# Weighting two heads in one VectorE instruction, with four buffers for counts and weighted tiles

## The chip, the cores and the metric

The kernel runs on one NeuronCore of one Trainium2 chip. The time is the device time of one execution in microseconds; several executions are made and their median is given. The engines are named as in the profile: PE is TensorE (PEld its weight loads), DVE is VectorE, ACT is ScalarE, POOL is GpSimd, SP is SyncE, which issues the DMAs.

## What is computed

The reference is one layer over x of 16 sequences x 512 tokens x 128 channels, float32: a normalised and modulated input goes through a gathering convolution, then a mixture of 8 experts of which each token takes 2. The part that matters here is the convolution. Each token and each of 8 heads has a frequency and a phase, and takes 32 taps of the sequence at fractional positions, each weighted by an entry of a table of 64 bins that is computed from the token itself:

```python
offs = phase[..., None] + freq[..., None] * taps          # 32 taps
pos = jnp.clip(jnp.arange(L)[None, :, None, None] + offs, 0.0, L - 1)
i0 = jnp.floor(pos).astype(jnp.int32); frac = pos - jnp.floor(pos)
g0 = xh[b_idx, i0, h_idx]
g1 = xh[b_idx, jnp.minimum(i0 + 1, L - 1), h_idx]
gathered = g0 + frac[..., None] * (g1 - g0)
kmat = (x @ kernel_w.T + kernel_b).reshape(B, L, H, 64)
w = jnp.take_along_axis(kmat, bins, axis=3)               # bins from offs
y = jnp.einsum('blhs,blhsd->blhd', w, gathered)
```

After it come the output product, the residual, the second normalisation, the gate (softmax over the two best of 8 scores), the experts (silu(h1) * h2, then the second product) and the residual again.

## The kernel before

The kernel doesn't gather. For each token and head it forms a dense row over the 512 positions: how many taps lie below each position and how far the next one is, as a product of a few parameter rows with constants. This row is weighted by the token's bins and multiplied by the steps of the input along the sequence.

Sequences are worked in 8 pairs. A pair has 8 rounds (R counts them, r = R % 8), one for each residue of the token index; 128 partitions hold 64 tokens of each of the two sequences. A round has 8 heads (h), and one head of one round is a tile T, 512 in all. Tile T passes through these steps:

- TensorE, `tile_on(T)`: two bfloat16 products of 512 columns, `ps_n` (L984) and `ps_p` (L987), each with two PSUM banks. They wait until the count and the gap of tile T-2 have read the banks.
- ScalarE, `gap(T)`: Relu of `ps_p` with a scale for each token, into `ee` (L771), two buffers.
- VectorE, `counted(T)`: `dq = ps_n * 2^27 + ee`, rounded to int32 (L1291), two buffers.
- VectorE, `weighted(T)`: `aw = dq * ks` over 65 groups of 8 positions, 520 elements, where `ks` holds one weight for each group and is read with a stride of zero within the group (L1301). `aw` has three buffers (`RING`).
- TensorE, `turn_tile(T)`: four transposes of 128x128 into `ps_t` (L995), two banks.
- ScalarE, `tile_evicted(T)`: copy into `att` (L779).
- TensorE, `weigh(R, g)`: 16 products for four heads, into `ps_y` (L1015).

Each engine has its own queue, written out by hand, and semaphores between them. No engine goes round a waiting instruction. The order in which the loops issue, for each T:

- TensorE: `tile_on(T + 3)`, `turn_tile(T)`, then what belongs to this head: `counts` of the next round (h 0, L976), `bins` (h 1, L952) and `weigh` of the last round (h 1), `weigh_edges` (h 2, L1024), `weigh` (h 5), products of the neighbouring pairs of sequences at h 3, 5 and 7 (such as `waves`, L947, `scores`, L1042, `outputs`, L1034), and two `turn_edges` (h 7, L1002).
- ScalarE: `gap(T + 3)`, `tile_evicted(T)`, then `counted` (h 0, L761), `copied` (h 4, L794), groups of four normalising activations (L729) at r 1 and 2, h 0 and 2, evictions of side products (L714, L739, L743, L748) at h 0, 4 and 6, and two `edge_evicted` (h 7, L786).
- VectorE: `counted(T + 1)`, `weighted(T)`, then `binned` (h 3, L1281), `edge_terms` (h 5, L1310) and the statistics, scores and masks of the neighbouring pairs of sequences.
- SyncE loads `ks` for round R + 2 once all weightings of round R are done; GpSimd pads bins, finishes normalisations and scatters rows, its scatters paced by the count of weightings (`s_aw`).

Two waits of VectorE matter for the change. `counted(T)` waits for `s_aw >= T - 1`, that is for the weighting of tile T-2, since it writes the same `dq` buffer. `weighted(T)` waits for the transposes of tile T-3, which read the same `aw` buffer.

After the head loop the expert stage runs over 135 slot tiles and the results are fetched and stored. It uses `aw` as space for other tiles.

Of the kernel before, what the change touches and what calls it, by code (L numbers as in the profile page):

```python
# [5 lines left out]
HEADS, D, TAPS, BINS = 8, 16, 32, 64  # L6
P = 128
# [7 lines left out]
NG = L // 8 + 1  # L15
NX = 8 * NG
# [4 lines left out]
ROWS = 32  # L21
QUAD = P // ROWS
KRING = 4
RING = 3
AHEAD = 3
SCALE = 2.0 ** 27
EXPERTS, FF = 8, 256
# [48 lines left out]
UNIT = {tag: n for n, tag in enumerate(ORDER)}  # L76
# [12 lines left out]
def build(nc, x, wave_wT, wave_b, kern_wT, kern_b, out_wT, w12T, w3T, gateT, cT, wmod,  # L89
          c_n, c_p, c_e, c_tok, c_ident, c_iota, c_tri, c_id, c_trash, c_tile, out):  # L90
    fp32, bf16, i32, u32 = mybir.dt.float32, mybir.dt.bfloat16, mybir.dt.int32, mybir.dt.uint32
    ALU, ACT, AX = mybir.AluOpType, mybir.ActivationFunctionType, mybir.AxisListType

    def rows(ap, extra):

        return bass.AP(ap.tensor, ap.offset, [list(ap.ap[0])] + [list(e) for e in extra])
# [12 lines left out]
    with ctx:  # L109
        def sb(name, shape, dt=fp32):  # L110
            return ctx.enter_context(nc.sbuf_tensor(name, shape, dt))
# [4 lines left out]
        def sem(name):  # L116
            return ctx.enter_context(nc.semaphore(name))
# [49 lines left out]
        ka = sb("ka", [P, 2, HEADS, PADK])  # L167
        ks = sb("ks", [P, 2, HEADS, NG])
        ee = sb("ee", [P, 2, 512])
        dq = sb("dq", [P, 2, NX], i32)  # L170
        aw = sb("aw", [P, RING, NX])
        att = sb("att", [P, SLOTS, 512])
        yt = sb("yt", [P, RES, HALF * P])
# [63 lines left out]
        ps_n, ps_p, ps_t, ps_y, side = ps[0:2], ps[2:4], ps[4:6], ps[6], ps[7]  # L237
# [18 lines left out]
        s_dq, s_aw, s_at, s_ev, s_y, s_yy = (sem("tap_count_ready"), sem("weighted"), sem("turned"), sem("evicted"),  # L256
                                             sem("y_product"), sem("y_copied"))
# [629 lines left out]
        def _(pe):  # L887
# [101 lines left out]
            def turn_tile(T):  # L989
# [3 lines left out]
                for j in range(NJ):  # L993
                    o = RES - r + j * P
                    last = nc.tensor.transpose(bank[:, j * P:j * P + P], aw[:, T % RING, o:o + P], ident[:, :])  # L995
                last.then_inc(s_at, 1)
# [179 lines left out]
        def _(dve):  # L1176
# [16 lines left out]
            for a in (2, 5):  # L1193
                g = mod[:, a * C:a * C + C]
# [13 lines left out]
            def deviation(which, done):  # L1208

                fence()  # L1210
                for r in range(RES):
                    ins = nc.vector.bn_aggr(mv[:, which, r, :], stats[:, which, r, :])
                link(ins)
                nc.vector.tensor_tensor(var[:, which, :], rows(mv[:, which, 0, 1:2], [[2, RES]]), tiny[:, :], ALU.add).then_inc(done, 1)

            def first_spread(i, n):
                if n == 0:
                    dve.wait_ge(s_xl, 16 * (i + 1))
                    if i:
                        dve.wait_ge(s_h, i)  # L1220
                spread(0, xc[:, i % 3, :], n)

            def second_spread(i, n):
                dve.wait_ge(s_xo, 2 * i + n + 1)
                spread(1, xo[:, :, :].rearrange("p r c -> p (r c)"), n)
# [37 lines left out]
            def waves(i):  # L1263
                dve.wait_ge(s_sd, SIDE["wave", i] + 1)
                nc.vector.tensor_tensor(wv[:, :, :], side[:, 0:RES * 16].rearrange("p (r w) -> p r w", w=16),
                                        rows(wbias[:, :], [[0, RES], [1, 2 * HEADS]]), ALU.add).then_inc(s_wv, 1)

            def periods(i):
                dve.wait_ge(s_tanh, i + 1)
                half = (MAX_FREQ - MIN_FREQ) / 2  # L1270
                f = freq[:, :, :].rearrange("p r h -> p (r h)")
                link(nc.vector.scalar_tensor_tensor(f, f, half, middle[:, :], ALU.mult, ALU.add))
                nc.vector.reciprocal(rows(x3[:, 0, 0:1], [[3, TILES]]), f).then_inc(s_fa, 1)

            def binned(R):
                dve.wait_ge(s_sd, SIDE["bins", R] + 1)
                if R >= KRING:
                    dve.wait_ge(s_kf, R - KRING + 1)
                    dve.wait_ge(s_kst[(R - KRING) % RES], 16 * ((R - KRING) // RES) + 16)
                    dve.wait_ge(s_kd, R - KRING + 1)  # L1280
                nc.vector.tensor_tensor(kn[:, R % KRING, :, LO:LO + BINS], side[:, :].rearrange("p (h k) -> p h k", k=BINS),  # L1281
                                        kbias[:, :].rearrange("p (h k) -> p h k", k=BINS), ALU.add).then_inc(s_kn, 1)

            def counted(T):

                o = RES - T // HEADS % RES
                dve.wait_ge(s_n, T + 1)
                dve.wait_ge(s_e, T + 1)
                if T >= 2:
                    dve.wait_ge(s_aw, T - 1)  # L1290
                nc.vector.scalar_tensor_tensor(dq[:, T % 2, o:o + 512], ps_n[T % 2][:, :], SCALE, ee[:, T % 2, :], ALU.mult, ALU.add).then_inc(s_dq, 1)  # L1291

            def weighted(T):

                R, h = T // HEADS, T % HEADS
                if h == 0:
                    dve.wait_ge(s_ksl[R % 2], 32 * (R // 2 + 1))
                dve.wait_ge(s_dq, T + 1)
                if T >= RING:
                    dve.wait_ge(s_at, UNIT["tile", T - RING] + 1)  # L1300
                nc.vector.tensor_tensor(aw[:, T % RING, :].rearrange("p (g k) -> p g k", k=8), dq[:, T % 2, :].rearrange("p (g k) -> p g k", k=8),  # L1301
                                        rows(ks[:, R % 2, h, 0:1], [[1, NG], [0, 8]]), ALU.mult).then_inc(s_aw, 1)

            def edge_terms(R):

                dve.wait_ge(s_ev, UNIT["count", R] + 1)
                dve.wait_ge(s_kd, R + 1)
                if R >= 2:
                    dve.wait_ge(s_est[R % 2], 32 * (R // 2))
                nc.vector.tensor_tensor(kr[:, R % 2, :], en[:, R % 2, :], kd[:, R % 2, :], ALU.mult).then_inc(s_kr, 1)  # L1310

            def scaled(i, n):

                dve.wait_ge(s_sd, SIDE["out", i, n] + 1)
                dve.wait_ge(s_modld, 32 * (i + 1))
                if i:
                    dve.wait_ge(s_xo, 2 * i + n - 1)
                else:
                    dve.wait_ge(s_modst, 16)
                nc.vector.tensor_tensor(hn[:, 4 * n:4 * n + 4, :], side[:, :].rearrange("p (r c) -> p r c", c=C),  # L1320
                                        rows(mb[:, 2, :], [[0, 4], [1, C]]), ALU.mult).then_inc(s_hn, 1)
# [34 lines left out]
            for T in range(NT):  # L1356
                i, R, r, h = T // TILES, T // HEADS, T // HEADS % RES, T % HEADS
                last, more = i - 1, i + 1 < PAIRS
                if T + 1 < NT:
                    counted(T + 1)  # L1360
                weighted(T)
                if h == 3 and R + 2 < NR:
                    binned(R + 2)
                if h == 5 and R + 1 < NR:
                    edge_terms(R + 1)
                if more:
                    if (r, h) == (0, 1):
                        first_spread(i + 1, 0)
                    if (r, h) == (0, 2):
                        first_spread(i + 1, 1)  # L1370
                    if (r, h) == (0, 6):
                        deviation(0, s_rs1)
                    if (r, h) == (3, 1):
                        waves(i + 1)
                    if (r, h) == (3, 6):
                        periods(i + 1)
                if i:
                    if (r, h) == (0, 7):
                        scaled(last, 1)
                    if (r, h) == (1, 2):  # L1380
                        second_spread(last, 1)
                    if (r, h) == (1, 4):
                        deviation(1, s_rs2)
                    if (r, h) == (4, 0):
                        scores(last)
                    if (r, h) == (4, 2):
                        choices(last)
                    if (r, h) == (4, 4):
                        masks(last)
                    if (r, h) == (5, 1):  # L1390
                        ranks_read(last)
                    if (r, h) == (5, 2):
                        spotted(last, 0)
                    if (r, h) == (5, 3):
                        spotted(last, 1)
                if (r, h) == (7, 1):
                    scaled(i, 0)
                if (r, h) == (7, 5):
                    second_spread(i, 0)
# [27 lines left out]
            for k, d in enumerate((1, 2, 4)):  # L1427
                a, b = upto[:, k % 2, :], upto[:, 1 - k % 2, :]
# [44 lines left out]
            for f in range(PAIRS):  # L1473
                s = f % 2
# [74 lines left out]
```

## Time and profile before

| | us |
|---|---|
| median of three executions | 1491.42 |
| lowest and highest | 1490.12, 1495.94 |
| the profiled execution | 1488.08 |
| its span, first to last instruction | 1486.3 |
| TensorE busy in the span | 1196.9 |
| VectorE | 1049.9 |
| ScalarE | 924.4 |
| GpSimd | 718.3 |

The span is that of one profiled execution, and all durations are from it. Matmuls are pipelined and their ends are modelled, so the busy time of TensorE overstates its work. Idle time of an engine is listed ahead of the instruction that ended it, with what released it. The granted clock is a share of 2.4 GHz.

### The profile page before, as it was taken

The numbers are of one execution on the slowest core, as the hardware profiler recorded it, in microseconds if no ns is written. First come the engines' busy times: TensorE is split into PE (matmuls) and PEld (weight loads), VectorE is DVE, ScalarE is ACT, GpSimd is POOL, SyncE is SP. The second block draws the span as 40 slices with busy tenths as digits, with TensorE's granted clock in tenths as the row PEclk, the third lists the DMA queues.
The fourth block names the chain that finished last, engine by engine and source line by source line (L and its number), as shares of the span: only waits on it lengthen the run. The fifth ranks groups of instructions, "written<-read, shape, count | busy, mean of one in ns | idle before, by whom it ended". The sixth has DMA issues, their size and how long they took to land.

```text
span 1486.3 us, 35019 instructions
## 1 busy us (share of the span) xinstructions
PE 1196.9 (81%) x11339; PEld 769.4 (52%) x11339; DVE 1049.9 (71%) x2314; ACT 924.4 (62%) x1905; POOL 718.3 (48%) x930
## 2 busy tenths in 40 slices
PE   0589988898899898898989988898992399999950
PEld 0346655555565555555555555555652155565530
DVE  1388798888978887888888798878884233333336
ACT  0277777777677777777677777777770155555530
POOL 4253146348536644753573476255243645455430
PEclk9999999999999999999999999999996699999985
DMA  5345434544443454445445444544351253222227
GB/s 160 112 127 139 119 100 135 151 108 136 129 136 106 130 145 116 125 133 136 114 127 149 115 108 121 148 115 115 109 148 56 70 160 95 73 73 69 73 90 281
DMA packets 208737, 180.22 MB, mean 121 GB/s; under 512 B 147633, under 2 KB 177201, under 8 KB 208177
## 3 DMA queue, kind: packets, MB, share of 16 engines
q1 hardware_dynamic: 199888, 160.07, 38.4%
q0 software_dynamic: 8672, 17.92, 3.6%
q8 instruction: 96, 1.57, 0.5%
q14 instruction: 81, 0.66, 0.1%
HBM read 95.81 MB, written 82.12 MB: 120 GB/s over the span
## 4 chain that ended last, share of the span: by engine, by line
PE 47%; DVE 18%; issue 14%; ACT 9%; POOL 7%; DMA 4%; SPq 1%; DVEq 0%; ACTq 0%; POOLq 0%
DVE aw L1301 9%; PE ps L995 8%; PE ps L1138 7%; PE ps L1015 6%; PE ps L984 4%; ACT att L779 4%; PE ps L1153 3%; PE ps L987 3%; DVE dq L1291 3%; PE ps L952 3%; POOL slot_scratch L570 2%; ACT ee L771 2%; PE ps L1002 2%; PE ps L1145 2%; DMA att<-y_scratch 1%
## 5 line engine op out<-in xcount | busy, mean ns | idle before, releaser
L771 ACT ACTIVATE ee<-ps,f 128x512 f32<-128x512 f32 x512 | 354.7, 693 | 202.9 <-PE ps L987 200.6
L1291 DVE SCALAR_TENSOR_TENSOR dq<-ps,ee 128x512 int32<-128x512 f32 x512 | 352.7, 689 | 135.7 <-ACT ee L771 83.5
L1301 DVE TENSOR_TENSOR aw<-dq,ks 128x520 f32<-128x520 int32 x512 | 415.3, 811 | 1.2 <-DMA ks<-k_scratch 1.2
L995 PE MATMUL ps<-ident,aw 128*128 128x128 f32 x2048 | 323.2, 281 | 49.7 <-DVE aw L1301 30.6
L995 PEld LDWEIGHTS ps<-ident,aw 128*128 128x128 f32 x2048 | 237.6, 142 | 221.0 <-DVE aw L1301 132.1
L779 ACT ACTIVATE att<-ps 128x512 f32<-128x512 f32 x512 | 308.1, 602 | 21.2 <-PE ps L995 20.8
L984 PE MATMUL ps<-cn,ptt 128*128 128x512 bf16 x512 | 199.9, 390 | 38.9 <-DVE dq L1291 38.1
L601 POOL COPY kn<-kn 128x256 f32<-128x256 f32 x64 | 25.4, 397 | 390.9 <-DVE kn L1281 390.9
L987 PE MATMUL ps<-cp,ptt 128*128 128x512 bf16 x512 | 196.7, 384 | 0.0
L701 POOL DMA_INDIRECT y_scratch<-aw,idu x135 | 129.2, 957 | 129.3 <-ACT aw L875 128.1
L570 POOL DMA_INDIRECT slot_scratch<-hrow,spotu x128 | 133.6, 1044 | 81.2 <-DVE aw L1301 47.5
L1453 DVE TENSOR_TENSOR aw<-ee,ps 128x256 f32<-128x256 f32 x135 | 56.8, 421 | 136.6 <-ACT ee L862 135.6
L862 ACT ACTIVATE ee<-ps 128x256 f32<-128x256 f32 x135 | 51.7, 383 | 152.9 <-PE ps L1138 152.9
L1015 PE MATMUL ps<-att,dl 128*32 128x128 f32 x4096 | 143.5, 282 | 0.8
L1138 PE MATMUL ps<-kn,ee 128*128 x270 | 143.1, 612 | 0.1
L1015 PEld LDWEIGHTS ps<-att,dl 128*32 128x32 f32 x4096 | 107.7, 112 | 60.1 <-ACT att L779 36.4
L786 ACT ACTIVATE att<-ps 128x512 f32<-128x512 f32 x128 | 74.4, 599 | 48.2 <-PE ps L1002 47.9
L984 PEld LDWEIGHTS ps<-cn,ptt 128*128 128x128 bf16 x512 | 49.8, 97 | 98.5 <-DVE dq L1291 68.3
L1002 PE MATMUL ps<-ident,ka 128*128 128x128 f32 x512 | 76.0, 278 | 14.4 <-ACT att L779 14.0
L1153 PE MATMUL ps<-hg,aw 128*128 x540 | 82.5, 275 | 0.1
L1132 PE MATMUL ps<-ident,dl 128*128 128x128 f32 x135 | 38.3, 283 | 54.8 <-DMA dl<-slot_scratch 32.5
L608 POOL TENSOR_TENSOR kd<-kn 128x504 f32<-128x504 f32 x64 | 77.5, 1212 | 0.0
(175 smaller groups left out, 1689.8 us busy)
## 6 DMA issues: line engine op xcount, KB each, us to landing
k_scratch<-kn SPq DMA_DIRECT2D x64, 512.0 KB, 2.6
ka<-e_scratch SPq DMA_DIRECT2D x64, 512.0 KB, 3.9
ks<-k_scratch SPq DMA_DIRECT2D x128, 130.0 KB, 4.3
e_scratch<-kr SPq DMA_DIRECT2D x128, 126.0 KB, 3.5
dl<-slot_scratch SPq DMA_DIRECT2D x135, 65.0 KB, 1.8
att<-y_scratch SPq DMA_DIRECT2D x16, 512.0 KB, 5.1
xc<-in_x SPq DMA_DIRECT2D x8, 512.0 KB, 5.9
h_scratch<-hx SPq DMA_DIRECT2D x8, 512.0 KB, 5.1
```

The lines of the kernel that those rows point to most:

```text
L570: pool.indirect_dma_start(out=slots[:, :], out_offset=bass.IndirectOffsetOnAxis(ap=spotu[:, k * RES + r:k * RES + r + 1], axis=0), in_=hro ...
L701: pool.indirect_dma_start(out=yscr[:, :], out_offset=bass.IndirectOffsetOnAxis(ap=idu[:, s:s + 1], axis=0), in_=yrow[:, y, :], in_offset=N ...
L771: act.activation(ee[:, T % 2, :], ps_p[T % 2][:, :], ACT.Relu, scale=f27[:, i % 2, r, h:h + 1]).then_inc(s_e, 1)
L779: act.activation(att[:, h, :], ps_t[UNIT["tile", T] % 2][:, :], ACT.Copy).then_inc(s_ev, 1)
L984: nc.tensor.matmul(ps_n[T % 2][:, :], p, cn[:, h % QUAD, :], start=True, stop=True).then_inc(s_n, 1)
L987: nc.tensor.matmul(ps_p[T % 2][:, :], p, cp[:, h % QUAD, :], start=True, stop=True).then_inc(s_p, 1)
L995: last = nc.tensor.transpose(bank[:, j * P:j * P + P], aw[:, T % RING, o:o + P], ident[:, :])
L1015: last = nc.tensor.matmul(ps_y[ROWS * k:ROWS * k + ROWS, g * P:g * P + P], dl[:, R // RES % 2, j, h, :], att[:, h, j * P:j * P + P], start ...
L1138: nc.tensor.matmul(ps_h[j % 2][:, :], xT[:, j % 2, :], w12[:, bass.ds(experts[j % 8] * (2 * FF), 2 * FF)], start=True, stop=True).then_inc ...
L1153: last = nc.tensor.matmul(ps_z[j % 2][:, 0:C], hidT[:, j % 2, k * P:k * P + P], w3[:, bass.ds(experts[j % 8] * (HALVES * C) + k * C, C)], ...
L1291: nc.vector.scalar_tensor_tensor(dq[:, T % 2, o:o + 512], ps_n[T % 2][:, :], SCALE, ee[:, T % 2, :], ALU.mult, ALU.add).then_inc(s_dq, 1)
L1301: nc.vector.tensor_tensor(aw[:, T % RING, :].rearrange("p (g k) -> p g k", k=8), dq[:, T % 2, :].rearrange("p (g k) -> p g k", k=8), rows( ...
```

## The change

The weighting of an even tile and that of the following odd tile become one instruction, issued at the odd tile. `dq` has four buffers instead of two, `aw` four instead of three; with an even tile in slot s the odd one is in slot s + 1, so the pair is one access pattern, and `ks` is read for heads h and h + 1. The waits follow: the count of tile T waits for the weighting of tile T-4 (`s_aw >= T - 3`), the double weighting waits for the counts of both tiles and for the transposes of the tile four before the later one. The counter of weightings rises by two at once. TensorE, ScalarE, GpSimd and SyncE have the same instructions in the same order.

```diff
-RING = 3
+RING = 4
...
-        dq = sb("dq", [P, 2, NX], i32)
+        dq = sb("dq", [P, RING, NX], i32)
...
-                if T >= 2:
-                    dve.wait_ge(s_aw, T - 1)
-                nc.vector.scalar_tensor_tensor(dq[:, T % 2, o:o + 512], ps_n[T % 2][:, :], SCALE, ee[:, T % 2, :], ALU.mult, ALU.add).then_inc(s_dq, 1)
-
-            def weighted(T):
-
-                R, h = T // HEADS, T % HEADS
+                if T >= RING:
+                    dve.wait_ge(s_aw, T - RING + 1)
+                nc.vector.scalar_tensor_tensor(dq[:, T % RING, o:o + 512], ps_n[T % 2][:, :], SCALE, ee[:, T % 2, :], ALU.mult, ALU.add).then_inc(s_dq, 1)
+
+            def weighted_two(T):
+
+                R, h, s = T // HEADS, T % HEADS, T % RING
                 if h == 0:
                     dve.wait_ge(s_ksl[R % 2], 32 * (R // 2 + 1))
-                dve.wait_ge(s_dq, T + 1)
+                dve.wait_ge(s_dq, T + 2)
                 if T >= RING:
-                    dve.wait_ge(s_at, UNIT["tile", T - RING] + 1)
-                nc.vector.tensor_tensor(aw[:, T % RING, :].rearrange("p (g k) -> p g k", k=8), dq[:, T % 2, :].rearrange("p (g k) -> p g k", k=8),
-                                        rows(ks[:, R % 2, h, 0:1], [[1, NG], [0, 8]]), ALU.mult).then_inc(s_aw, 1)
+                    dve.wait_ge(s_at, UNIT["tile", T + 1 - RING] + 1)
+                nc.vector.tensor_tensor(aw[:, s:s + 2, :].rearrange("p a (g k) -> p a g k", k=8), dq[:, s:s + 2, :].rearrange("p a (g k) -> p a g k", k=8),
+                                        rows(ks[:, R % 2, h, 0:1], [[NG, 2], [1, NG], [0, 8]]), ALU.mult).then_inc(s_aw, 2)
...
                 if T + 1 < NT:
                     counted(T + 1)
-                weighted(T)
+                if T % 2:
+                    weighted_two(T - 1)
```

## Rows read from the trace of the kernel before

**Rows 1.** Stretch: length; busy us PE, PEld, DVE, ACT, POOL; clock; DMA share; GB/s.

```profile
350.00:500.00 150.00, 131.53 (x1386) 83.72 (x1384) 127.81 (x254) 110.53 (x215) 85.73 (x112) 0.98 0.46 131
```

**Rows 2.** Line L1301 alone: ns min/median/max, first and last start.

```profile
L1301 DVE TENSOR_TENSOR aw<-dq,ks x512: 682/690/2804, 68.7 to 1113.0; 128x520 f32<-128x520 int32 x171
```

**Rows 3.** Groups of instructions by line: busy us, mean ns, idle before, releaser.

```profile
L1301 DVE TENSOR_TENSOR aw<-dq,ks 128x520 f32<-128x520 int32 x512 | 415.3, 811 | 1.2 <-DMA ks<-k_scratch 1.2
...
L1291 DVE SCALAR_TENSOR_TENSOR dq<-ps,ee 128x512 int32<-128x512 f32 x512 | 352.7, 689 | 135.7 <-ACT ee L771 83.5 <-PE ps L984 26.0 <-DVE aw L1301 0.5
...
L1310 DVE TENSOR_TENSOR kr<-en,kd 128x504 f32<-128x504 int32 x64 | 57.3, 895 | 11.1 <-ACT en L761 11.1
```

**Rows 4.** Timeline of VectorE: start us, length us, instruction.

```profile
1099.48 0.69 DVE L1291 SCALAR_TENSOR_TENSOR dq<-ps,ee 128x512 int32<-128x512 f32 x1
1100.09 0.69 DVE L1301 TENSOR_TENSOR aw<-dq,ks 128x520 f32<-128x520 int32 x1
1100.91 0.69 DVE L1291 SCALAR_TENSOR_TENSOR dq<-ps,ee 128x512 int32<-128x512 f32 x1
```

**Rows 5.** Groups of VectorE with 256 and 512 elements a partition.

```profile
L1453 DVE TENSOR_TENSOR aw<-ee,ps 128x256 f32<-128x256 f32 x135 | 56.8, 421 | 136.6 <-ACT ee L862 135.6 <-issue 1.0
...
L1281 DVE TENSOR_TENSOR kn<-ps,kbias 128x512 f32<-128x512 f32 x64 | 43.7, 683 | 4.3 <-PE ps L952 4.3
```

**Rows 6.** Timeline of several engines: how one instruction hands over to the next.

```profile
640.89 0.39 PE L984 MATMUL ps<-cn,ptt 128*128 128x512 bf16 x1
...
641.53 0.69 ACT L771 ACTIVATE ee<-ps,f 128x512 f32<-128x512 f32 x1 [1.54 <-PE ps L987]
...
641.89 0.66 PE L995 MATMUL ps<-ident,aw 128*128 128x128 f32 x4 [0.40 <-DVE aw L1301]
...
642.58 0.86 DVE L1301 TENSOR_TENSOR aw<-dq,ks 128x520 f32<-128x520 int32 x1
642.59 0.60 ACT L779 ACTIVATE att<-ps 128x512 f32<-128x512 f32 x1 [0.37 <-PE ps L995]
...
643.08 0.59 ACT L714 ACTIVATE ht<-ps 128x512 f32<-128x512 f32 x1
...
643.49 0.66 PE L995 MATMUL ps<-ident,aw 128*128 128x128 f32 x4 [0.17 <-DVE aw L1301]
...
643.99 1.86 PE L947 MATMUL ps<-ww,ht 128*128 128x16 f32 x16
...
651.73 0.69 ACT L771 ACTIVATE ee<-ps,f 128x512 f32<-128x512 f32 x1 [1.68 <-PE ps L987]
...
652.50 0.69 DVE L1291 SCALAR_TENSOR_TENSOR dq<-ps,ee 128x512 int32<-128x512 f32 x1 [0.64 <-ACT ee L771]
...
653.11 1.10 DVE L1301 TENSOR_TENSOR aw<-dq,ks 128x520 f32<-128x520 int32 x1
```

**Rows 7.** Timeline: work of even heads that isn't a tile's own.

```profile
648.38 0.62 ACT L761 ACTIVATE en<-ps 128x504 int32<-128x504 f32 x1
...
652.06 0.65 PE L1024 MATMUL ps<-att,hg 128*32 128x128 f32 x16
...
652.63 0.39 PE L984 MATMUL ps<-cn,ptt 128*128 128x512 bf16 x1
...
655.64 0.39 ACT L794 ACTIVATE yt<-ps 128x256 f32<-128x256 f32 x1
...
611.58 0.89 ACT L729 ACTIVATE hx<-xc,shift,rstd 128x128 f32<-128x128 f32 x2
```

**Rows 8.** Stretches of 4 us, columns as in rows 1.

```profile
618.00:622.00 4.00, 2.17 (x14) 1.11 (x17) 3.97 (x10) 2.23 (x5) 3.92 (x6) 0.88 0.34 135
622.00:626.00 4.00, 3.74 (x41) 2.11 (x41) 3.79 (x5) 1.86 (x4) 3.92 (x3) 0.69 0.37 65
...
670.00:674.00 4.00, 2.44 (x15) 1.21 (x14) 3.93 (x9) 2.95 (x7) 2.43 (x6) 1.00 0.54 175
```

**Rows 9.** Timeline of TensorE in the dip of rows 8.

```profile
620.92 1.06 PE L995 MATMUL ps<-ident,aw 128*128 128x128 f32 x4 [0.98 <-DVE aw L1301]
```

## The prediction

> **What bounds the kernel now.** I read the busy time by stretches first, then the groups of instructions, then the timeline of a few microseconds. The stretches [rows 1] show four engines that are all well filled: in 150 us of the head loop TensorE is busy 131.5, VectorE 127.8, ScalarE 110.5. No engine is full, so the question is what each waits for. The head loop runs from 68.7 to 1113.0 us [rows 2], 512 head tiles in 1044.3 us, 2.04 us each, 16.35 us for a round of eight heads. Only this part of the span can change; setup and the expert stage, some 440 us, contain no line of the diff's that does work of size.
>
> VectorE has two instructions in each tile: the count (`dq`, 689 ns) and the weighting (`aw`, 811 ns mean, 690 ns median) [rows 2, 3]. The timeline [rows 4] shows how close they follow each other: the weighting starts 0.61 us after the count, the next count 0.82 us after the weighting. The second is longer because `dq` has two buffers: the count of tile T+1 overwrites the buffer of tile T-1, whose weighting is the instruction just ahead, and waits for its end. So a tile costs VectorE at least 1.43 us, eight cost 11.4. The mean weighting lies 0.12 above its median, some 1.0 us for eight; the edge terms add 0.9 [rows 3], the bins 0.7 [rows 5], the rest of VectorE's work about 1.2. That is 15.2 of 16.35 us: VectorE is the nearest thing to a bound, and the shallow `dq` is part of it. This speaks for the change.
>
> **What it takes from VectorE.** With four `dq` buffers the count of T+1 waits for a weighting that is at least two tiles old: 0.82 - 0.61 = 0.21 us saved at each tile. Two weightings become one of 1040 elements a partition. No row shows that length. Nearest are 256 and 512 elements at 421 and 683 ns [rows 5], 1.02 ns an element, so 0.69 + 520 x 1.02 / 1000 = 1.22 us; I take 1.23. The bounds are 1.22 and twice the single, 1.38. It occupies VectorE for 0.61 + 0.54 = 1.15 us. A pair of tiles then costs VectorE 0.6 + 0.6 + 1.15 = 2.36 instead of 2.86 us: 0.5 us less, 128 us over 256 pairs, if VectorE set the pace afterwards.
>
> The Trainium skill (VectorE: DVE Perf Modes, the section on the errata) says that a fixed latency is paid once by each instruction and that fewer, larger ones spread it, with about 150 cycles as the fixed part; as an estimate from that page one merge saves some 0.16 us, 40 us in all. By the trace it is less: instructions start 0.61 us apart though each takes 0.69 [rows 4], so merging two leaves only 0.06 to 0.07 us to be saved.
>
> **What it puts on the path.** The weighted tile T-1 (T odd) is now delivered together with tile T, behind the count of T+1. TensorE works in order: transposes of T-1, count and gap products of T+3, transposes of T. It stands at the transposes of T-1 until the double weighting ends; only after them come the products of T+3. But the next double weighting stands on VectorE behind the count of T+3, which needs exactly those products and ScalarE's gap of T+3. That closes a ring through three engines in which two tiles pass per turn. Before, the same ring ran over a single weighting and three tiles passed per turn, so it had slack. Deeper `dq` and `aw` don't open it: neither buffer is what anyone in it waits for.
>
> One turn of the ring, from rows:
> - double weighting and handing over: 1.23 + 0.06 = 1.29 us. (A single that started at 642.58 and took 0.86 was followed by its transposes at 643.49, 0.05 later [rows 6].)
> - transposes of T-1 to the next TensorE work: 0.50 (643.49 to 643.99) [rows 6], up to 0.59; I take 0.53. Product of T+3 to ScalarE's gap: 0.64 (640.89 to 641.53) [rows 6]. Together 1.17. On ScalarE the eviction of T-1 stands ahead of that gap: it starts 0.70 after the transposes and releases ScalarE 0.49 later [rows 6]. So ScalarE's side is 1.19; I take 1.20.
> - gap to count 0.77, count to weighting 0.61 (651.73, 652.50, 653.11) [rows 6]: 1.38.
>
> Sum 3.87 us for two tiles with nothing else in the way. The weightings' excess over the median, 0.12 each, appears where GpSimd works at the same time; it lies wholly on the ring. Kept as it is it would be 0.24 a pair; VectorE will weigh for a smaller share of the time, so I take 0.20 (bounds 0.10 and 0.30). 4.07 us a pair, 256 pairs: 1042 us. Already equal to the whole loop of today.
>
> Whatever stands between the transposes of an even head and the products of T+3, on TensorE or on ScalarE, is now added in full:
> - each round: the counts at head 0 with their eviction on ScalarE (0.62 us long, about 0.5 of occupation) 0.5 us; the edge weights at head 2, 0.57 us (652.06 to 652.63); the copy at head 4, 0.39 us long, about 0.3 [rows 7]. 1.35 us, 64 times: 86 us.
> - each pair of sequences on ScalarE: four groups of four normalising activations, two in 0.89 us [rows 7], so 1.65 a group, less 0.55 in the two groups that stand at head 2: 5.5 us; ten evictions of side products at even heads, 0.5 each: 5.0; a tanh 0.2. 10.7 us, in seven of eight: 75 us.
> - TensorE's extras at odd heads have room: behind the transposes of T it is free at 1.45 us of the turn and needed again, products of T+4 included, at 4.07. One group of about 1.9 us (643.99, 1.86 [rows 6]) plus two edge transposes of 1.0 overruns by 0.8; there are four such places: 3.2 us, eight times, 26 us.
> - VectorE's extras must fit into 1.5 us between double weighting and count of T+3. Edge terms and bins do; three or four places for each pair of sequences overrun by some tenths, about 2.2 us: 18 us.
>
> These four are coarse; I bound their sum of 205 us by 0.6 and 1.3 times itself.
>
> Loop after: 1042 + 86 + 75 + 26 + 18 = 1247 us against 1044.3: +203. Filling and draining the ring: +1. Larger `dq` to clear on GpSimd in setup: nothing, since GpSimd waits there for the constants behind it anyway; 1 to 2 us without that cover. The counter of weightings moves by two; its readers compare with even numbers or one or two tiles of lag (SyncE's load of `ks`, GpSimd's paced scatters), nothing on the ring.
>
> **TensorE's clock.** It stands at 0.98 of 2.4 GHz in the 150 us [rows 1]. At 618 to 622 us TensorE was busy 2.17 of 4 us and the granted clock was 0.88, then 0.69 in the next four, on the way to the 1.2 GHz level and back; at 670 to 674, busy 2.44 of 4, it stayed at 1.00 [rows 8]. In a plain pair of the new loop TensorE's transposes and products are busy about 2.5 of 4.07 us (twice 0.60 from first product to end of second, twice 0.66 [rows 6]), plus the extras. That is near the weaker of the two rows, so there will be more dips. In that dip four transposes took 1.06 us [rows 9] instead of 0.66 [rows 6], 0.4 more; the products of T+3 should lose as much again, so I estimate up to +0.9 us a turn at the low level. I put 10 us into the sum for dips and leave the rest to a rival.
>
> Forecast: 1486.3 + 203 + 1 + 10 = 1700 us of span; about 2 us lie between span and time of the profiled execution (1488.08), and the median shown, 1491.42, is 3.3 above it. Within the coarseness of the terms I say 1700 us.
>
> **Rivals.**
> (a) VectorE is the bound and the ring is hidden. For it: 15.2 of 16.35 us a round. Then up to 128 us go: 1363 us, or some 1400 if TensorE takes over. It decides if the ring's turn is under 3.8 us with its extras; the rows give 4.07 without. It would need the products of T+3 ahead of the transposes of T-1, and the code has them behind. By the Trainium skill's rule of the fixed latency (same section as above) alone the time would be about 1450. Chance 0.07.
> (b) Gain and ring cancel: the extras of even heads hide in the ring after all, and the excess of the weightings vanishes: 256 x 3.87 = 991 plus about 50. 1490 us, within 0.5%. 0.03.
> (c) The clock falls for long stretches: half of the turns at the 1.2 GHz level cost 128 x 0.9 = 115 us more, all of them 230. 1815 to 1930 us. 0.10. Against it: no idle stretch of TensorE in a turn is much over 2 us. The Trainium skill (TensorE: Matmul & The Clock Gate) says that inactivity brings the slow state and activity the fast one; the rows at 618 to 626 us agree.
> (d) The double instruction costs twice the single, 1.38, or more with its extra dimension: +0.15 a turn, +38 us: 1740. It is inside the forecast's range, not a case of its own.
>
> **How the numbers follow.** Forecast (the ring sets the pace) 0.80, (a) 0.07, (b) 0.03, (c) 0.10. The range for 8 in 10 leaves out (a), (b) and most of (c). Low end: excess 0.10 a turn (-26), extras at 0.6 (-82): 1592, taken as 1600. High end: excess 0.30 (+26), extras at 1.3 (+62): 1788, taken as 1800 for a part of (d)'s 38. Half a per cent, 7 us, is about what a measurement of this kernel can tell from no change. Faster 0.07, same 0.03, slower 0.90.
>
> **What would show it.** In the profile after: 256 weightings of 1040 elements, median near 1.23 us. VectorE's busy time in 150 us down from 128 to about 98, its idle time ahead of the count, now on ScalarE's gap, up by far. TensorE's idle time ahead of the transposes, released by the weighting, up from 132 us (weight loads) to over 300, at even heads; hardly any at odd heads. Starts of successive double weightings 4 to 4.1 us apart where GpSimd and ScalarE have nothing extra, 4.9 on average. The chain of waits runs weighting, transposes, products, gap, count. I am wrong if these starts lie under 3.8 us apart, if VectorE stays over 120 of 150 us busy, or if the granted clock is well under 0.9 through the loop.

## The result and the profile after

The changed kernel takes 1677.04 us (median; 1675.45 to 1677.88), the kernel before 1492.66 us in the same comparison. The ratio is 1.1233, with a 95% interval of 1.1207 to 1.1258: slower by 12.3%, 184 us. The forecast was 1700 us in a range of 1600 to 1800.

The loss lies in the head loop. The line of the double weighting shows it (lengths in ns: least, median, largest; then the first and last start in us):

```profile
L1301 DVE TENSOR_TENSOR aw<-dq,ks x256: 1229/1231/2575, 69.0 to 1301.4; 128x1040 f32<-128x1040 int32 x128
```

The loop now lasts from 69.0 to 1301.4, 1232.4 us, against 1044.3 before [rows 2]: 188 us more, about the whole loss of 190 in span (1675.9 against 1486.3). 256 weightings are 4.83 us apart on average, where two tiles took 4.09.

The same stretch of 150 us as in [rows 1], with the same columns:

```profile
350.00:500.00 150.00, 117.32 (x1221) 76.94 (x1209) 104.26 (x188) 95.39 (x182) 66.34 (x90) 0.94 0.41 110
```

In a stretch of the same length every engine is less busy than before: TensorE 117.3 instead of 131.5 us, VectorE 104.3 instead of 127.8, ScalarE 95.4 instead of 110.5. A kernel that gets slower while all its engines get idler has a new wait. The groups of instructions say where (busy us, mean ns, then idle time ahead of them and what ended it):

```profile
L1291 DVE SCALAR_TENSOR_TENSOR dq<-ps,ee 128x512 int32<-128x512 f32 x512 | 353.4, 690 | 351.4 <-ACT ee L771 192.6 <-issue 103.1 <-PE ps L984 53.7
L1301 DVE TENSOR_TENSOR aw<-dq,ks 128x1040 f32<-128x1040 int32 x256 | 349.7, 1366 | 0.1
L995 PE MATMUL ps<-ident,aw 128*128 128x128 f32 x2048 | 339.0, 291 | 229.0 <-DVE aw L1301 219.8 <-ACT att L779 1.8
...
L995 PEld LDWEIGHTS ps<-ident,aw 128*128 128x128 f32 x2048 | 246.6, 147 | 413.9 <-DVE aw L1301 324.2 <-issue 52.6
```

VectorE stands 351 us ahead of counts (136 before, [rows 3]), and 193 of them end with ScalarE's gap (84 of 136 before). TensorE stands 220 us ahead of the transposes until a weighting ends. In the kernel before these were 31 us, and 132 for the weight loads, which are now at 324:

```profile
PEld ps L995 <- DVE aw L1301: 132.1, 218, 1.5
```

VectorE waits for ScalarE, ScalarE for TensorE, TensorE for VectorE. One turn of that ring can be read off the timeline of the changed kernel, at the start of a round:

```profile
808.48 1.23 DVE L1301 TENSOR_TENSOR aw<-dq,ks 128x1040 f32<-128x1040 int32 x1
...
809.76 0.66 PE L995 MATMUL ps<-ident,aw 128*128 128x128 f32 x4 [0.29 <-DVE aw L1301]
...
810.47 0.38 PE L984 MATMUL ps<-cn,ptt 128*128 128x512 bf16 x1
...
810.95 0.58 ACT L761 ACTIVATE en<-ps 128x504 int32<-128x504 f32 x1
...
811.42 0.60 ACT L739 ACTIVATE ptt<-ps 128x512 bf16<-128x512 f32 x1
811.90 0.70 ACT L771 ACTIVATE ee<-ps,f 128x512 f32<-128x512 f32 x1
...
812.68 0.69 DVE L1291 SCALAR_TENSOR_TENSOR dq<-ps,ee 128x512 int32<-128x512 f32 x1 [1.66 <-ACT ee L771]
...
813.29 1.23 DVE L1301 TENSOR_TENSOR aw<-dq,ks 128x1040 f32<-128x1040 int32 x1
```

Double weighting to transposes 1.28 us, transposes to gap 2.14, gap to count 0.78, count to the next double weighting 0.61: 4.81 us. The second leg would be 1.20 without the eviction of the counts (L761) and a side eviction (L739), which stand on ScalarE ahead of the gap and add 0.94, nearly twice 0.5.

Turns with nothing else in the way are seen too. Two double weightings in a row of the changed kernel:

```profile
841.88 1.23 DVE L1301 TENSOR_TENSOR aw<-dq,ks 128x1040 f32<-128x1040 int32 x1
...
845.73 1.23 DVE L1301 TENSOR_TENSOR aw<-dq,ks 128x1040 f32<-128x1040 int32 x1
```

The 3.85 us between them are the floor of the loop: of the 255 distances one is shorter (2.83, at the loop's very end), 12 lie between 3.85 and 3.87, and 116 between 4.25 and 4.65, which is the floor and one piece of side work. Without the excess of the weightings the prediction's sum for a turn is 3.87.

### The profile page after: what moved, and what is told of

It is laid out like the page before. It is cut to its first block and busy times, and to the rows that moved or that the text cites. A ratio compares the mean times of both kernels' runs of the same rounds, so it can differ in the third digit from the quotient of the medians.

```text
span 1675.9 us, 34571 instructions
## 1 busy us (share of the span) xinstructions
PE 1232.5 (74%) x11339; PEld 803.5 (48%) x11339; DVE 1013.3 (60%) x2058; ACT 934.8 (56%) x1905; POOL 691.4 (41%) x930
## 5 line engine op out<-in xcount | busy, mean ns | idle before, releaser
L995 PE MATMUL ps<-ident,aw 128*128 128x128 f32 x2048 | 339.0, 291 | 229.0 <-DVE aw L1301 219.8
L995 PEld LDWEIGHTS ps<-ident,aw 128*128 128x128 f32 x2048 | 246.6, 147 | 413.9 <-DVE aw L1301 324.2
L1301 DVE TENSOR_TENSOR aw<-dq,ks 128x1040 f32<-128x1040 int32 x256 | 349.7, 1366 | 0.1
L984 PE MATMUL ps<-cn,ptt 128*128 128x512 bf16 x512 | 204.2, 399 | 0.7 <-DVE dq L1291 0.7
L987 PE MATMUL ps<-cp,ptt 128*128 128x512 bf16 x512 | 202.2, 395 | 0.0
L1015 PE MATMUL ps<-att,dl 128*32 128x128 f32 x4096 | 160.6, 305 | 7.5 <-ACT yt L794 6.7
L1015 PEld LDWEIGHTS ps<-att,dl 128*32 128x32 f32 x4096 | 121.2, 122 | 72.9 <-ACT att L779 52.4
L1145 PEld LDWEIGHTS ps<-ident,aw 128*128 128x128 f32 x270 | 38.1, 141 | 72.0 <-issue 46.8
L1153 PEld LDWEIGHTS ps<-hg,aw 128*128 128x128 f32 x540 | 70.9, 191 | 0.3 <-issue 0.3
```

Of the source, the lines that this page charges most:

```text
L984: nc.tensor.matmul(ps_n[T % 2][:, :], p, cn[:, h % QUAD, :], start=True, stop=True).then_inc(s_n, 1)
L987: nc.tensor.matmul(ps_p[T % 2][:, :], p, cp[:, h % QUAD, :], start=True, stop=True).then_inc(s_p, 1)
L1015: last = nc.tensor.matmul(ps_y[ROWS * k:ROWS * k + ROWS, g * P:g * P + P], dl[:, R // RES % 2, j, h, :], att[:, h, j * P:j * P + P], start ...
L1153: last = nc.tensor.matmul(ps_z[j % 2][:, 0:C], hidT[:, j % 2, k * P:k * P + P], w3[:, bass.ds(experts[j % 8] * (HALVES * C) + k * C, C)], ...
L1301: nc.vector.tensor_tensor(aw[:, s:s + 2, :].rearrange("p a (g k) -> p a g k", k=8), dq[:, s:s + 2, :].rearrange("p a (g k) -> p a g k", k= ...
```

## The experiments

The theory is the ring of the prediction. Against it stand: the double instruction is itself too costly; the lower clock is the cause; the load of an engine sets the pace; the deeper buffers do the harm. Times are medians, and the interval is that of the ratio to the kernel before, measured beside each. Beside buffers_alone, two_singles, ahead4 and buffers_ahead4 the kernel before took 1503.97 us, beside the others 1490.46 to 1492.66, so between these groups ratios are to be compared, not times. In the traces of those four kernels it is the stage behind the head loop that is longer, 382 to 385 us against 373 to 376 in all others, and no line of any edit works there. The last column has the head loop of the profiled execution, from the first weighting's start to the last one's; it is 1044.3 us in the kernel before.

| kernel | us | ratio to before | 95% | head loop, us |
|---|---|---|---|---|
| the change | 1677.04 | 1.1233 | 1.1207 to 1.1258 | 1232.4 |
| buffers_alone | 1513.32 | 1.0064 | 1.0041 to 1.0088 | 1060.7 |
| two_singles | 1603.62 | 1.0641 | 1.0602 to 1.0680 | 1149.5 |
| ahead4 | 1549.25 | 1.0293 | 1.0267 to 1.0318 | 1097.5 |
| buffers_ahead4 | 1537.30 | 1.0219 | 1.0192 to 1.0245 | 1075.9 |
| dummy_behind | 1680.80 | 1.1273 | 1.1243 to 1.1302 | 1232.5 |
| dummy_ahead | 1802.98 | 1.2088 | 1.2060 to 1.2115 | 1354.8 |
| pe_again | 1668.81 | 1.1175 | 1.1146 to 1.1205 | 1225.3 |
| centred_odd | 1641.19 | 1.1000 | 1.0972 to 1.1028 | 1195.4 |
| before_dummy | 1530.26 | 1.0272 | 1.0250 to 1.0293 | 1084.0 |
| before_pe_again | 1526.93 | 1.0250 | 1.0229 to 1.0271 | 1081.5 |
| before_centred | 1485.72 | 0.9970 | 0.9959 to 0.9982 | 1040.8 |
| ahead4_centred | 1547.45 | 1.0391 | 1.0362 to 1.0421 | 1099.3 |

### The same work on and off the ring

One small VectorE instruction (256 elements, its result unused) for each pair, at two places that are one line apart: `dummy_behind` has the line below the weighting, `dummy_ahead` the line above it. The diff shows both; the allocation of the tile `dum` and its clearing in setup are left out.

```diff
                 if T % 2:
+                    nc.vector.tensor_tensor(dum[:, 1, :], dum[:, 0, :], dum[:, 0, :], ALU.mult)   # only in dummy_ahead
                     weighted_two(T - 1)
+                    nc.vector.tensor_tensor(dum[:, 1, :], dum[:, 0, :], dum[:, 0, :], ALU.mult)   # only in dummy_behind
```

> The changed kernel with one more VectorE instruction per pair (256 elements, about 0.42 us long, 0.33 to 0.36 us of its queue), right behind the double weighting. Theory of the ring: it falls into the 1.5 us in which VectorE waits for the count's gap; only pairs that also hold edge terms or bins feel it: 0 to 25 us over the changed kernel, about 1688. Rival, that VectorE's load sets the pace: 256 x 0.35 = 90 us more, about 1767.

> The same additional instruction, but between the count of T+1 and the double weighting, on the ring. Theory of the ring: all of it is added to each turn: 80 to 90 us over the changed kernel, about 1762. Rival, VectorE's load: the same 90 us, so only the difference from the kernel with the instruction behind the weighting tells the two apart: 65 us or more by the ring, none by the load.

The groups of the two kernels, `dummy_behind` first:

```profile
L1365 DVE TENSOR_TENSOR dum<-dum 128x256 f32<-128x256 f32 x256 | 132.4, 517 | 0.0
```

```profile
L1364 DVE TENSOR_TENSOR dum<-dum 128x256 f32<-128x256 f32 x256 | 144.4, 564 | 0.0
```

Behind the weighting, instructions of 132 us in sum are added (they overlap with their neighbours; VectorE's busy time in the loop rises by 95 us), and 4 us show by the times, 6 by the ratios, whose intervals overlap. Ahead of it, 144 us are added and the kernel takes 7.6% more than the change by the ratios, 126 us by the times. So VectorE's load doesn't set the pace of the changed kernel, and what stands between the count and the double weighting does. It is paid in full: the double weighting starts 0.33 us after the additional instruction in the typical case and 0.48 on average, 123 us in sum, and the loop is 122 us longer. The shortest distance of two double weightings, leaving out the last one, goes from 3.85 to 4.19 us. The 80 to 90 us expected were too few because they were worked out from the typical length: the median is 0.42, as assumed, but the mean 0.56. The granted clock of the same 150 us fell to 0.89 as well. Not much is left for it: the double weightings took 1323 ns on average instead of 1366, 11 us less in sum, so of the loop's 122 us some 10 could be the clock's (an estimate: 122 - 123 + 11). The stretch in `dummy_ahead`:

```profile
350.00:500.00 150.00, 111.02 (x1048) 72.14 (x1046) 106.34 (x193) 87.19 (x164) 63.78 (x86) 0.89 0.35 98
```

### The ring opened on TensorE's and ScalarE's side

```diff
-AHEAD = 3
+AHEAD = 4
```

> The changed kernel with products and gaps issued four tiles ahead instead of three, on TensorE and ScalarE. The products of T+3 then stand ahead of the transposes of T-1, so that the next double weighting no longer hangs on the last one. Theory of the ring: the loss is gone and VectorE's saving shows: about 1420 us, 1380 to 1470. Rival, that the double instruction or the granted clock is the cause: 1640 or more, for neither is touched.

One constant removes three quarters of the loss: 12.3% becomes 2.9%, with the double instruction untouched, its length unchanged (mean 1359 ns), and a granted clock that is little higher (0.97 against 0.95 in the loop, 0.925 against 0.914 in the span; with 0.99 in the loop `pe_again`, below, gained some 9 us). The floor of 3.85 us is gone with it: 78 of the 255 distances between double weightings lie under 3.8 us, the shortest at 2.75. (The starts at 143.20 and 146.14 are such a pair.) TensorE's longest waits for VectorE are now of two kinds and of similar size, where the changed kernel had 324 us of one:

```profile
PEld ps L984 <- DVE dq L1291: 95.6, 92, 1.9
...
PEld ps L995 <- DVE aw L1301: 83.6, 76, 1.9
```

But it didn't come below the kernel before, as I had expected (1380 to 1470). The gain that was to appear behind the ring isn't there, and the expectation missed by 79 us at its near end.

### The parts by themselves

Four buffers with one weighting per tile in the old order; then the same with four tiles ahead.

```diff
-RING = 3
+RING = 4
...
-        dq = sb("dq", [P, 2, NX], i32)
+        dq = sb("dq", [P, RING, NX], i32)
...
-                if T >= 2:
-                    dve.wait_ge(s_aw, T - 1)
+                if T >= RING:
+                    dve.wait_ge(s_aw, T - RING + 1)
...
```

The lines left out index `dq` by `T % RING` where it is written and read.

> One part of the change alone: four buffers each for dq and aw, one weighting per tile in the old order. Theory of the ring (in the changed kernel the double weighting of a pair is followed, in order, by transposes, products, gap, count and the next double weighting; two tiles pass per turn): here the ring has slack as before, and VectorE no longer waits for its own last weighting, 0.21 us a tile. At most 107 us are saved, other engines take up part: about 1440 us, 1400 to 1475. Rival, that the deeper buffers themselves do the harm (addresses, setup): at or above 1500.

> Four buffers each, one weighting per tile, products and gaps four tiles ahead. It tells whether the earlier products are worth something by themselves. Theory of the ring: with single weightings the ring had slack, so little is added to the four buffers alone: within 20 us of that kernel, about 1430. Rival, that any earlier issue of products helps, whatever the weightings: over 30 us below it.

Both expectations failed. Nothing was saved where 16 to 91 us under the kernel before were forecast, and the earlier products cost 24 us where within 20 was said. The condition of the first one's rival, 1500 us or more, is met in figures, but the kernel before took 1504 beside it: the deeper buffers do harm, by 0.6% of the 12.3%. It isn't in the setup: the first weighting starts at 68.3 us, before at 68.7. The four buffers do what they should: a count starts 0.60 us after the weighting ahead of it, where it was 0.82 [rows 4]. Timeline of `buffers_alone`:

```profile
563.82 0.68 DVE L1301 TENSOR_TENSOR aw<-dq,ks 128x520 f32<-128x520 int32 x1
564.42 0.68 DVE L1291 SCALAR_TENSOR_TENSOR dq<-ps,ee 128x512 int32<-128x512 f32 x1
```

Two tiles follow each other in as little as 2.41 us, where it was 2.85 (once 2.71). Yet nothing is won in sum. A quiet round (one with little work for other pairs of sequences), the kernel before first, then `buffers_alone`:

```profile
542.40:557.30 14.90, 13.80 (x160) 8.71 (x158) 13.18 (x27) 11.88 (x22) 4.68 (x7) 1.00 0.55 147
```

```profile
549.70:564.40 14.70, 13.62 (x159) 8.80 (x159) 13.02 (x28) 11.63 (x22) 4.65 (x7) 1.00 0.55 148
```

This round gains 0.2 us. TensorE is busy for 13.8 of 14.9 us, the most of all engines; that what VectorE gets ready earlier waits for TensorE is read from this and not tried. The stretches that lose are rounds with much side work. The next two lines cover rounds R = 33 and 34, from the eviction of counts (L761) of R = 33 to that of R = 35, before first:

```profile
611.00:648.40 37.40, 31.16 (x305) 19.20 (x304) 32.06 (x51) 28.91 (x60) 28.65 (x31) 0.95 0.43 126
```

```profile
619.00:658.70 39.70, 33.60 (x306) 21.36 (x304) 32.32 (x52) 29.40 (x60) 29.69 (x32) 0.87 0.44 129
```

The same 305 matmuls take 2.4 us more of TensorE's time at a granted clock of 0.87 instead of 0.95. So a dip of the clock goes along with the loss; whether it is its cause or follows from another rhythm of waits was not tried. The two traces are also from different comparisons, in which the kernel before took 1491 and 1504 us, so a part of the difference may not be the edit's. Four tiles ahead cost single weightings another 1.5%, about 23 us. That helps to read `ahead4`: of its 2.9%, 0.6 and 1.5 come with buffers and early products, and the pairing that made 12.3% is worth 0.7 there.

The pair in two instructions, at the place of the double one, against the changed kernel (`weighted` is the single weighting of before, with four buffers):

```diff
                 if T % 2:
-                    weighted_two(T - 1)
+                    weighted(T - 1)
+                    weighted(T)
```

> The changed kernel, but the pair is weighted by two single instructions, T-1 and then T, at the place of the double one. Theory of the ring: the transposes of T-1 start 0.54 us earlier in each turn, so 256 x 0.54 = 138 us less than the changed kernel: about 1540 us, 1520 to 1580; still slower than before, since the weighting of T-1 is still behind the count of T+1. Rival, that the double instruction itself is what costs (its length, its meeting with GpSimd's work): 1491 us or less, as all of it is gone. Rival, that only the amount of VectorE's work counts: about 0.06 us more per pair than changed, 1690.

5.3% less than the change by the ratios, 88 us, not 138; the expected range of 1520 to 1580 was missed. The direction speaks for the ring: the double instruction is gone and the kernel is still 6.4% slower than before, 5.7% slower than with the same buffers and the same instructions in the old order. The shortest turns speak for it too: the first weightings of two pairs follow each other in as little as 3.31 us (as at 350.48 and 353.79; the last pair, 2.73, left out), 0.54 less than the floor of the change, as the sum says. But the loop of 1149.5 us makes 4.50 for a pair, 0.33 less than in the change. So longer turns gained less than the short ones, and which path takes the other 0.21 there was not traced.

### The clock and TensorE's load

The four transposes of each odd tile are done twice, in both kernels.

```diff
-                for j in range(NJ):
+                for j in [*range(NJ)] * (1 + T % 2):
```

> The changed kernel with the four transposes of each odd tile done twice (the second time with the same result), 0.44 us more TensorE work per pair at a place where it later waits. Theory of the ring: the work itself costs nothing. If the lower granted clock of the changed kernel (0.94 in the loop instead of 0.99) has a share in the loss, the busier TensorE holds the clock up and the time falls, by 5 to 30 us: about 1660, mean clock of the loop over 0.96. Rival, TensorE's load: 113 us more, 1790.

> The kernel before with the four transposes of every odd tile done twice, 0.44 us more for TensorE per pair. In the changed kernel this cost nothing. If TensorE bounds the kernel before, most of 256 x 0.44 = 113 us show: 1560 to 1600. If VectorE bounds it, under 40 us: about 1520.

In the changed kernel, some 113 us of additional TensorE work (256 times 0.44) make it 0.5% faster, about 9 us, and the granted clock of the loop rises from 0.95 to 0.99, which is what the kernel before has. The whole loops, the change first, then `pe_again`:

```profile
69.00:1301.40 1232.40, 962.87 (x9903) 628.78 (x9903) 849.70 (x1470) 782.09 (x1476) 498.99 (x703) 0.95 0.39 107
```

```profile
69.60:1294.90 1225.30, 1025.63 (x10923) 719.75 (x10923) 841.19 (x1469) 795.88 (x1475) 496.44 (x702) 0.99 0.39 108
```

The stretch of 150 us would mislead here. It rises from 0.94 to 0.98, but it also stands at 0.98 in `dummy_behind`, which gained nothing and has 0.96 in its loop. Over the span, all four executions of `pe_again` have 0.945 to 0.960 and those of the change 0.914 to 0.932. The intervals of the two ratios lie side by side (1.1146 to 1.1205, 1.1207 to 1.1258), so the gain is small. It is also a net one: what the repeated transposes cost by themselves isn't known, and so the clock's share in the 184 us is about 9 us plus that cost. The Trainium skill (TensorE: Matmul & The Clock Gate, the section on what is actually happening) states that the default state is throttled and that activity releases the throttle; the rise from 0.95 to 0.99 with busier TensorE agrees.

In the kernel before, the same work costs 2.5%, 37 of 113 us. By its expectation that is the side on which VectorE, not TensorE, bounds the kernel (under 40 us); the next run says that VectorE doesn't either.

### How near VectorE was to a bound

The dummy instruction of above, in the kernel before, behind every second weighting.

```diff
                 weighted(T)
+                if T % 2:
+                    nc.vector.tensor_tensor(dum[:, 1, :], dum[:, 0, :], dum[:, 0, :], ALU.mult)
```

> The kernel before with the additional VectorE instruction (256 elements) behind every second single weighting. My prediction held VectorE for the nearest thing to a bound of the kernel before. If so, most of the instruction's time shows: 256 x 0.35 to 0.45 us = 90 to 115, about 1590. Rival, that TensorE's order bounds the quiet rounds and VectorE only the rounds with much side work: 20 to 60 us, about 1530.

2.7%, 40 us, as the rival said (20 to 60). VectorE's busy time in the loop rose by 93 us, from 887.6 to 980.3, and less than half of it shows. With the 37 of 113 us for TensorE, neither engine alone bounds the kernel before. That each takes the lead in a part of the rounds fits both figures; no run took the rounds apart.

### ScalarE's groups moved off the ring

```diff
-                    if (r, h) == (2, 0):
+                    if (r, h) == (2, 1):
                         centred(1, last, 0)
-                    if (r, h) == (2, 2):
+                    if (r, h) == (2, 3):
                         centred(1, last, 1)
...
-                    if (r, h) == (1, 0):
+                    if (r, h) == (1, 1):
                         centred(0, i + 1, 0)
-                    if (r, h) == (1, 2):
+                    if (r, h) == (1, 3):
                         centred(0, i + 1, 1)
```

> The changed kernel with ScalarE's four groups of normalising activations per pair of sequences moved from heads 0 and 2 to heads 1 and 3, behind the eviction of the odd tile, off the ring. Theory of the ring, by the price in the prediction: 5.5 us for seven of eight pairs of sequences, 38 us less than the changed kernel: 1639, 1625 to 1660. Rival, ScalarE's load: no change.

> The kernel before with the four groups of normalising activations moved from heads 0 and 2 to heads 1 and 3. Control for the same move in the changed kernel, which gave 36 us. Theory of the ring: the gain belongs to the ring; where three tiles pass per turn there is room for them: within 10 us of the kernel before. Rival, that the move is good in any order: 20 us or more below it.

> The changed kernel with products and gaps four tiles ahead and the normalising activations moved to heads 1 and 3. If four tiles ahead have opened the ring, ScalarE's groups at even heads no longer stand on it: within 8 us of the kernel with four tiles ahead, about 1550. If a part of the ring is left, 20 us or more below it, about 1520.

The prediction priced these groups at 38 us; moving them by one head gives 2.3 points of the ratio, 36 us by the times and 37 in the loop. No work was removed. In the kernel before the same move gives 0.3%, 5 us. So the price belongs to the ring. With four tiles ahead the time is the same, 1547 us against 1549, while the ratio is one point higher, as the kernel before was faster in that comparison. The loops of the two traces are 1099.3 and 1097.5 us. A gain of 20 us is excluded, a small loss isn't. `before_centred` is the fastest kernel measured here, by little, and has nothing of the change.

## Why the prediction was right

- **The double instruction**: 1.23 us taken, 1.231 measured. The bound of 1.38 was too wide.
- **The ring**: right, with its order, and shown by the two dummies (4 against 126 us) and by the one constant that opens it. The legs were 1.29, 1.20 and 1.38; the turn above has 1.28, 2.14 with extras that were priced separately, and 1.39. A turn without side work and without excess was summed to 3.87 us and measures 3.85.
- **Excess of the weightings**: 0.20 us a pair taken, 1.366 - 1.231 = 0.135 measured, 17 us less in 256 pairs. With it the loop's sum of 1247 becomes 1230; measured are 1232. The other terms hold in sum. Of the single ones only ScalarE's groups were measured, 36 against 38; that the rest, coarse by the prediction's own words, comes out within 2 us in sum is in part luck.
- **The clock**: dips were named and 10 us put in. The granted clock of the loop fell from 0.99 to 0.95, and a net 9 us came back with a busier TensorE. I had counted it on top of the loop's 203; the loop's 188 contain it. With the 17 us of the excess this is why 1700 was forecast and 1677 came.
- **VectorE as the nearest bound** was the step that failed. It was summed to 15.2 of 16.35 us a round, and 0.21 us a tile was said to be lost by the shallow `dq`. The 0.21 are there, but removing them made the kernel 0.6% slower, and of 93 us more VectorE work 40 show. The sum mixed quiet rounds, in which TensorE leads (13.8 of 14.9 us), with rounds full of side work. For the forecast it didn't matter, since the ring went past every engine. Rival (a), with 1363 to 1400 us, rested on this step.
- **The Trainium skill's rule** (VectorE: DVE Perf Modes, the section on the errata) that merging saves the fixed latency would have given some 40 us less by the prediction's estimate. The lengths agree with it: 2 x 0.690 - 1.231 = 0.149 us by the medians, 38 us in 256 pairs, where the estimate from the page was 0.16 and 40. With the smaller excess the weightings' time fell by 415.3 - 349.7 = 66 us. But the rule says nothing on who waits for the first half of the merged result, and that is where the time went.
- **Signs foretold**: VectorE busy about 98 of 150 us (104.3), weight loads of the transposes over 300 us idle (324), starts 4.9 us apart on average (4.83). Starts 4 to 4.1 us apart with nothing extra were foretold and hardly occur (none from 4.00 to 4.10, 5 of 255 up to 4.15): the excess comes on 45 of the 256 double weightings and not as 0.20 on each, so plain turns take 3.85. The transposes wait at even heads alone, as foretold: each of the 228 waits of their weight loads ends with the end of a double weighting. The chain of waits was to show the ring; its view of the changed kernel covers only the last 23% of the span, from 1286 us on, so all but the loop's last turns is missing.

## What to carry to other kernels

Before merging two instructions of a software pipeline, follow the first of the merged results: whoever reads it now waits for the second input too. If, in some engine's fixed order, the producer of that second input stands behind that reader, a ring is closed, and more buffers for the merged tensors don't open it (here four each didn't); the order does. Its turn can be added up from the timeline, leg by leg, and everything that stands on a leg is paid in full, while the same work one place further is free. A wait of an engine for its own last result is no promise either: here its removal brought nothing, as neither this engine's load nor TensorE's alone set the pace.

## What the runs showed that I had not expected

- A deeper buffer that removed a real wait of 0.21 us made the kernel 0.6% slower (1.0041 to 1.0088), with a granted clock of 0.87 instead of 0.95 in two rounds that lost.
- Some 113 us more TensorE work left the changed kernel no slower (1.1175 against 1.1233) and raised the granted clock of its loop from 0.95 to 0.99.
- Issuing the products one tile earlier, which opens the ring, costs 1.5% where there is no ring (1.0064 to 1.0219). Why stays open.
- A VectorE instruction with both inputs in SBUF was stretched only beside GpSimd's work. In `dummy_behind` the 256-element instruction takes 0.42 us in the median, as one with an input in PSUM does [rows 5], and 0.52 on average: of 150 with no GpSimd instruction at the same time none took over 0.42, of 106 others 37 took 0.63 to 1.49. The weightings of the kernel before do the same: of 219 with none beside them none took over 0.70, of 291 others 131 took over 0.72, up to 2.80. That the one causes the other is inferred from this; no run moved GpSimd's work.
